# The middle block as one sequence of slots, with the second layer norm and router product inside

## What is computed

```python
x = x + 0.5 * _L0_ffn_ref(_layernorm(x), router_w, w1, w2)
x = x + _L0_attn_ref(_layernorm(x), W_in, conv_w, conv_b, dt_bias, A_log, D, norm_weight, W_out)
x = x + 0.5 * _L0_ffn_ref(_layernorm(x), router_w, w1, w2)
```

```python
zxbcdt = x @ W_in                       # z 512, xBC 512 + 2 * 64, dt 8
xBC = _silu(conv(xBC, conv_w, 4 taps) + conv_b)
dt = softplus(dt + dt_bias); dA = exp(dt * A)
# s = s * dA + dt * x B ; y = C s        over the tokens of a batch row
y = (y + D * x) * _silu(z)
y = y * rsqrt(mean(y * y) + EPS) * norm_weight
return y @ W_out
```

## Time and profile before

| | us |
|---|---|
| median of 3 runs | 1469.66 (1469.64 to 1472.97) |
| profiled execution | 1467.08 |
| its span, first to last instruction | 1465.0 |
| TensorE, DVE, ScalarE, GpSimd busy | 1127.1, 825.2, 573.7, 708.2 |
| mean granted TensorE clock | 0.85 |

### The profile page before, as it was taken

How to read it: one execution, slowest core, us unless ns; L and a number is a source line. 1 busy time by engine, 2 the same in 40 slices (tenths; PEclk the granted TensorE clock), 3 DMA queues, 4 the chain that set the end, 5 groups by cost and what they waited for, 6 DMA issues and landing times. The chain is left out here.

```text
span 1465.0 us, 23436 instructions
## 1 busy us (share of the span) xinstructions
PE 1127.1 (77%) x7002; PEld 940.2 (64%) x7034; DVE 825.2 (56%) x1721; ACT 573.7 (39%) x1375; POOL 708.2 (48%) x673
## 2 busy tenths in 40 slices
PE   3748999999177868686869696978494899999900
PEld 3737999999155746464647475655393799999900
DVE  6883444444266667667676767674448344444433
ACT  2313555555134333434344444353141455555500
POOL 7845555554115454554546363646314555555400
PEclk9999999999677969697969787887655899999965
DMA  7752222222310101010101010000291222222277
GB/s 237 237 215 69 77 77 76 77 78 58 99 33 22 37 12 33 23 32 25 32 26 32 18 36 22 26 8 8 89 318 60 69 78 77 78 77 77 58 226 243
DMA packets 77090, 116.26 MB, mean 79 GB/s; under 512 B 10416, under 2 KB 64192, under 8 KB 75712
## 3 DMA queue, kind: packets, MB, share of 16 engines
q1 hardware_dynamic: 52544, 64.68, 13.4%
q0 software_dynamic: 13824, 37.77, 8.4%
q10 hardware_dynamic: 10624, 12.58, 2.6%
HBM read 70.96 MB, written 44.04 MB: 78 GB/s over the span
## 5 line engine op out<-in xcount | busy, mean ns | idle before, releaser
L405 POOL DMA_INDIRECT ys_d<-xs,row_of x144 | 142.4, 989 | 194.8 <-DVE xs L790 184.3
L779 DVE TENSOR_TENSOR xl<-pT,xh 128x256 fp32r<-128x256 f32 x144 | 61.2, 425 | 210.6 <-ACT xh L485 116.6
L472 ACT ACTIVATE hs<-pH 128x512 f32<-128x512 f32 x144 | 86.2, 598 | 229.0 <-PE pH L582 219.0
L400 POOL DMA_INDIRECT xs<-xn_d,token_of x144 | 141.1, 980 | 52.2 <-issue 42.3
L784 DVE TENSOR_TENSOR h2l<-hs,h2h 128x512 fp32r<-128x512 f32 x144 | 99.9, 693 | 84.2 <-ACT h2h L480 77.8
L1281 PE MATMUL bank<-tri_bf,al 128*128 128x128 bf16 x768 | 62.3, 239 | 56.4 <-ACT ex L1173 56.4
L602 PE MATMUL pY<-w2h,h2h 128*128 x576 | 103.4, 301 | 0.5 <-DVE h2l L784 0.3
L1281 PEld LDWEIGHTS bank<-tri_bf,al 128*128 128x128 bf16 x768 | 52.9, 108 | 68.4 <-ACT ex L1173 65.5
L582 PE MATMUL pH<-w1h,xh 128*128 x288 | 93.1, 405 | 1.9 <-DVE xl L779 1.0
L602 PE MATMUL pY<-w2h,h2l 128*128 x576 | 92.0, 282 | 0.0
L602 PE MATMUL pY<-w2l,h2h 128*128 x576 | 91.7, 281 | 0.0
(11 more groups left out here) (243 smaller groups left out, 2789.5 us busy)
## 6 DMA issues: line engine op xcount, KB each, us to landing
xn_d<-xs SPq DMA_DIRECT2D x16, 512.0 KB, 3.4
m_yg<-ys_d SPq DMA_DIRECT2D x64, 128.0 KB, 2.1
xs<-ys_d SPq DMA_DIRECT2D x16, 512.0 KB, 6.1
wst<-in_L_ffn_w_dram ACTq DMA_DIRECT2D x8, 512.0 KB, 4.8
xs<-in_L_attn_x_dram SPq DMA_DIRECT2D x8, 512.0 KB, 7.0
hs<-in_L_ffn_w_dram ACTq DMA_DIRECT2D x8, 512.0 KB, 5.3
lo_d<-w1l SPq DMA_DIRECT2D x1, 4096.0 KB, 11.1
lo_d<-w2l SPq DMA_DIRECT2D x1, 4096.0 KB, 21.4
```

The source lines that it names most:

```text
L400: pool.indirect_dma_start(out=xg[:, t % NX, :], out_offset=None, in_=xn_d, in_offset=bass.IndirectOffsetOnAxis(ap=token_of[:, t:t + 1], ax ...
L405: pool.indirect_dma_start(out=ys_d, out_offset=bass.IndirectOffsetOnAxis(ap=row_of[:, t:t + 1], axis=0), in_=y[:, t % NX, :], in_offset=No ...
L472: act.activation(r[:, u, :], pH[u][:, :], ACT.Relu).then_inc(relu_done.sem, 1)
```

## The change

In the second FFN the first stage goes: `ffn_block` runs its loads, moments, normalisation, transposes, logits and copies only when `first` is set, and the loads of the low halves of the weights (`load_lo`) stand first in SP's queue. `logits` and `rwT` are kept from the first FFN on.

```diff
+            if not first:
+                for m in range(NA):
+                    load_lo(m)
+            if first:
                 for h in range(NA):
                     load(0, h, False)
...
-            else:
-                with pool.Fori(0, T // (2 * AG)) as j:
-                    pows(j, 0)
-                    pows(j, 1)
```

```diff
+PROJECTED = {3: (2, (0, 1)), 0: (1, (2,)), 1: (1, (3, 4))}
+TAPPED = {0: (1, (0, 1)), 1: (1, (2,)), 2: (1, (3, 4))}
+RX = 14
+LEAD = 10
...
+            for s in SLOTS:
+                first, late = blocks(s, PROJECTED)[:1], blocks(s, PROJECTED)[1:]
+                if live(s):
+                    from_state(s)
+                if live(s - 3):
+                    score(s - 3, s)
+                if live(s - 1):
+                    out_product(s - 1)
+                if live(s):
+                    within(s)
+                    to_state(s)
+                if live(s + 1):
+                    turn_b(s + 1)
+                    turn_xc(s + 1)
+                for B in first:
+                    project(*B, s)
+                if live(s):
+                    turn_y(s)
+                if live(s + 1):
+                    sums(s + 1, 0)
+                if live(s + 9):
+                    turn_x(s + 9)
+                if live(s + 2):
+                    project_z(s + 2)
+                if live(s + 1):
+                    sums(s + 1, 1)
+                for B in late:
+                    project(*B, s)
...
+                if live(s + 9):
+                    project_dt(s + 9)
+                if live(s - 2):
+                    turn_x2(s - 2, s)
```

```diff
+            for s in SLOTS:
+                if live(s):
+                    if not ends(s):
+                        decay_state(s)
+                    add_skip(s)
+                    gate_y(s)
+                if live(s + 1):
+                    scale_x(s + 1)
+                if rooted(s + 1):
+                    powers(s + 1)
+                for G, m in blocks(s, PROJECTED):
+                    if m in BY_POOL:
+                        add_tap(G, m)
```

Operations also change hands or place. ScalarE normalises x and the second norm's x, as scale and bias; DVE makes the bias (`shift`):

```diff
+                act.activation(xn[:, :], xr[:, i % RX, :], ACT.Identity, bias=nmr[:, q, 0:1], scale=rstd[:, q, 0:1]).then_inc(norm_done.sem, 1)
...
+                dve.scalar_tensor_tensor(nmr[:, q, :], mv[:, q, 0:2, 0], -1.0, rstd[:, q, 0:2], ALU.mult, ALU.mult).then_inc(nmr_done.sem, 1)
```

One power of three columns per slot takes the place of two of one column (first norm, second norm, norm of y). GpSimd adds tap 1 for two blocks of five instead of making it for four; DVE does tap 1 for the other three. The bias of dt is added once per group. The mask is made in place, and C B is first copied to SBUF:

```diff
-                dve.tensor_tensor(M[:, :, :], ex[:, :, :], pG.rearrange("p (a t) -> p a t", a=1).to_broadcast([P, H, P]), ALU.mult).then_inc(M_done.sem, 1)
...
+                act.activation(GB[:, :], pGB, ACT.Copy).then_inc(bt_done.sem, 1)
...
+                dve.tensor_tensor(ex[:, :, :], ex[:, :, :], GB[:, 0:P].rearrange("p (a t) -> p a t", a=1).to_broadcast([P, H, P]), ALU.mult).then_inc(M_done.sem, 1)
```

More of the change, by code:

```diff
@@ L513, in _ @@
                 s.open(pe)
[L514 to L538, removed]
-                for m in range(0, NA * AG, 2):
-                    if m + 2 < NA * AG:
-                        turn(m + 2)
-                        turn(m + 3)
-                    score(m)
-                    score(m + 1)
@@ new lines, in live, with blocks, rooted, blocks_before @@
+        def live(i):
+            return 0 <= i < T
+        def blocks(s, table):
+            if s % GC not in table:
+                return ()
+            ahead, places = table[s % GC]
+            G = s // GC + ahead
+            return tuple((G, m) for m in places) if 0 <= G < NG else ()
+        def rooted(s):
+            return live(s + 9) or live(s - 2) or live(s - 1)
+        def blocks_before(s):
+            return sum(len(blocks(n, PROJECTED)) for n in range(-LEAD, s))
+        def ends(i):
+            return (i + 1) % PER == 0
@@ new lines, in score, with within @@
+            def score(i, s):
+                pe.wait_ge(x2T_copied.sem, x2T_copied.done(i))
+                pe.wait_ge(raw_done.sem, raw_done.done(blocks_before(s) - 1))
+                pe.wait_ge(logit_copied.sem, logit_copied.done(i - 1))
+                product(pLog, [(xT2[:, k, :], rwT[:, k, :]) for k in range(KD)]).then_inc(logit_ready.sem, 1)
+            def within(i):
+                pe.wait_ge(xdt_done.sem, xdt_done.done(i))
+                pe.wait_ge(M_done.sem, M_done.done(i))
+                pe.wait_ge(t2_done.sem, t2_done.done(i - 1))
+                for h in range(H):
+                    last = pe.matmul(pY[:, h * HD:(h + 1) * HD], ex[:, h, :], xdt[:, h * HD:(h + 1) * HD], start=True, stop=True)
+                last.then_inc(y_ready.sem, 1)
@@ new lines, in convolve @@
+            def convolve(pieces):
+                for n in range(1, CONV):
+                    for G, m in pieces:
+                        if n == 1 and m in BY_POOL:
+                            dve.wait_ge(tap1.sem, tap1.done(pooled(G, m)))
+                            continue
+                        if n == 1:
+                            dve.wait_ge(tap0.sem, tap0.done(G * NB + m))
+                        elif not (n == 2 and m in BY_POOL):
+                            dve.wait_ge(tap_chain, tapped[G, m])
+                        b = ORDER[m]
+                        a = acc[:, G % 2, b, :]
+                        ins = dve.scalar_tensor_tensor(a, raw[:, b, n:n + GT], cwh[:, b, n:n + 1], a, ALU.mult, ALU.add)
+                        if n == CONV - 1:
+                            ins.then_inc(taps.sem, 1)
+                        else:
+                            ins.then_inc(tap_chain, 1)
+                            tapped[0] += 1
+                            tapped[G, m] = tapped[0]
```

1028 lines of the change are left out of this document (521 added, 507 removed).

## The result

The median is 1379.92 us (1379.43 to 1392.05, 4 executions) against 1469.65 us of before; the ratio is 0.9405, with a 95% interval of 0.9352 to 0.9458. So the change makes the kernel faster by 6%, where 1353 us, 8%, had been forecast. The profiled execution has a span of 1378.1 us (before 1465.0) and a mean granted clock of 0.88 (before 0.85).

A forecast was written before the change was run, and what follows sets the result against it. No engine was taken as full; the middle block's queue order was the limit. From 1467.1 us, 69.4 for the block and 47.1 for the second norm gave 1350.6, with the median's 2.6 us 1353; range 1300 to 1405 (8 in 10).

The forecast's parts named there:

- rival A: Middle block: DVE and TensorE bind in turn, group 62 to 70 us, total 1353 (1327 to 1380); chance 0.50.
- the lead: Ten lead slots before the first state product: it comes at 465 instead of 450.7, cost 14 us, bounds -5 and +25.
- the last slots: End of the block: slots 23 to 26 take 61 us, slots 27 to 31 take 59, the tail 5.
- Second norm, -47.1: Between block and second FFN: the norm stage of 49.5 us goes, iotas and a cast stay, gain 47.1 us.
- Norm inside the block: Per chunk, TensorE gains 0.6 us; per group ScalarE reaches 38 us, GpSimd falls to about 32, neither binding.
- The sums of the slots: Steady part, four slots per group: largest of TensorE, DVE and in-slot loop for each slot, summing to 64 us.
- kinds 3, 0, 1 and 2: Slots by s%4, with differing shares of the next groups' convolution; forecast 16.0, 17.6, 15.4 and 15.1 us.
- The clock, +2 per group: Steady slots: TensorE's waits behind slot 0 lower its clock, some 2 us lost, added once per group: 66 us.
- rival D: Block: waits recur, TensorE falls to the low level once per slot, 2 us each; 1392, up to 1430; chance 0.13.
- B: Block: the queues lose almost nothing, group 58 us, total 1301; chance 0.22.
- E: Block: TensorE stays at the low level, 1.8 times its time, 98 us per group, total 1561, slower; chance 0.04.
- Rival C: Block: GpSimd catches the mask in most slots, 1.2 us each, 4.9 per group, total 1385; chance 0.10.

The follow-up runs named there:

- e1: Changed kernel with the second norm and router product taken out of the slots, back to a stage behind the block; 1395.6 us.
- e3: Changed kernel with useless TensorE products ahead of the dt product, 5 in slots with s%4=0 and 8 in those with s%4=2; 1362.3 us.
- e11: Changed kernel with dt and router's products moved later, plus ten useless products ahead of L1242 in slots with s%4=1; 1344.2 us.
- e6: e3 with four more useless products ahead of the turning of y in slots with s%4=2; 1360.7 us.
- e10: e3 with 12 useless products in place of 8 ahead of the dt product in slots with s%4=2; 1354.1 us.
- e2: Changed kernel with the dt product moved to the next slot, behind the product of y with the output weights; 1374.6 us.
- e8: Changed kernel without GpSimd's product of x and D (D*x zero), with e3's useless products; median 1336.7 us.

## Why the prediction was right, and which term was mis-sized

The measured time lies in the range of 1300 to 1405, and at the very end of rival A's own (1380). What A named, slots set by TensorE and VectorE in turn with a wait that costs the clock, is what was found; the 27 us between forecast and median come in the main from one term, and the errors of the lead and of the last slots, 8 us each, happened to cancel.

- **Second norm, -47.1.** Right: -47.0. The low-half loads start behind the barrier (1008.14 to 1011.74) and cost nothing: from the first reduction to the end of the span it is 367.9 us, 368.9 before. The barrier gave 2 us more than the nothing that was counted.
- **Norm inside the block.** "Neither is the sum that binds" was said of ScalarE and GpSimd and holds. ScalarE has 37.7 us per group, 38 forecast, and GpSimd 37.3, not 32, with its scalings at 1.49 us for 1.04. For TensorE 0.6 us per slot was counted and 0.62 of busy time measured in the last slots (e1); the slots there are 0.84 us longer.
- **Lead.** 465 against 456.9. The ten lead slots cost 6 us more than before, not 14; if the bounds of -5 and +25 are those of the cost, it lies between them, as departures from 465 they are missed by 3 us.
- **The sums of the slots.** 16.0, 17.6, 15.4 and 15.1 us for kinds 3, 0, 1 and 2, 64 in all. At the full level e3 has 16.30, 16.66, 16.75 and 16.07 in slots 19, 16, 17 and 18: 65.8. The sum is 1.8 low. By kind it is off by +0.3, -0.9, +1.4 and +1.0, and slots 13 and 21 of e3, of kind 1, take 17.65, so that 3% is partly luck. The longest kind was to be 0, with 17.6 us of VectorE and 11.6 in kind 1; e3's slots 16 and 17 have 15.95 and 15.38. VectorE's sum was good (57.2; 58.1 per group in the kernel after), as was TensorE's (54.7; 55.8 in slots at 1.00: 13.43, 15.12 and 12.15 in slots 8, 13 and 10, 15.12 in e3's slot 7). e11, with a wholly different split (13.2, 20.0, 13.3 and 19.6), comes to 66.1; that this is the forecast's 66 is chance, as the forecast had 2 us of low level in it.
- **The clock, +2 per group: the term that failed.** Measured is 71.6 - 65.8 = 5.8 us per group. The prediction took one wait per group, and priced it by the products right behind it: "idle 2.59 us, then the pair of z products takes 1.20 us for 0.71", and "some 2 us lost". What follows a wait is not one or two products but some 16 us of them, from 573.79 to 590 in the timeline above, and TensorE, now busy for 90% of the time, has no slack to hide it. Six such slots of 23 are 3.5 to 5.9 us longer than e3's of the same kind at the full level, 29 us together, of the 33 us (5.75 x 5.8) that slots 0 to 22 take beyond e3's 65.8 per group. The step was right, that a wait for VectorE brings TensorE to its low level; the length was taken from two rows instead of from the whole stretch at that level, and the waits right ahead of the low slots were those for `xTl`, not those for the mask and y behind slot 0. The row that had it all was quoted under rival D: in the earlier trace rows the chunk that starts at 605.64 runs low and takes 16.7 us, its fellow k=1 11.7.
- **The rivals.** D (1392 to 1430) was half of the truth: the fall comes in a quarter of the slots, at 5 us, not in each at 2. B was out of reach: even e11, with nearly all slots at the full level, has 66 per group and not 58. E: in the kernel after, the low level never held for two slots in a row; its factor of 1.8 is 1.69 by the rows it names (1.20 for 0.71), which changes its 98 us per group to 92 and nothing else.
- **Rival C, the mask in SBUF.** It did not come: the mask takes between 1.20 and 1.23 us in all 32 cases. The reason given, that GpSimd waits at that time, holds for most of them. In seven, GpSimd's decay of S (L1032) lies beside the mask, and there it is GpSimd that pays: 1.6 to 1.9 us for an operation that takes 1.04 alone, and 2.7 to 2.8 in the three where VectorE's L1550, which also has two inputs in SBUF, stands right ahead of the mask. With the mask's old input in PSUM the same pair left each other alone, 21 times between 450 and 1000. Before, and after:

```profile
621.66 1.22 DVE L1518 TENSOR_TENSOR M<-ex,bank 128x1024 f32<-128x1024 f32 x1 [0.21 <-ACT ex L1173]
621.97 1.04 POOL L1074 TENSOR_TENSOR S<-S,dts 64x512 f32<-64x512 f32 x1
```

```profile
948.57 1.23 DVE L1557 TENSOR_TENSOR ex<-ex,GB 128x1024 f32<-128x1024 f32 x1 [3.11 <-ACT ex L1154]
948.81 1.89 POOL L1032 TENSOR_TENSOR S<-S,dts 64x512 f32<-64x512 f32 x1 [1.59 <-PE bank L1224]
```

So the copy of C B to SBUF did expose the mask, but the cost fell on GpSimd. In the cases read (614.96 and 948.81) GpSimd waited another 0.4 us for VectorE behind it, so that nothing was lost there. What the Trainium skill ("SBUF — State Buffer", section "Who interferes with whom") says of two SBUF inputs agrees with the taps (1.37 for 0.75 us) and with this pair.

- **What was to be seen.** No norm stage, first reduction 2.5 us behind the first iota, VectorE at 81%, taps above 0.75: yes. Period of 66, a clock of 0.9 and kind 0 as the longest: no (71.6, 0.85, and the slots at the low level).

## What to carry over

A slot sum that fills TensorE to 90% is not finished until each wait of TensorE has been followed through: price a wait by the whole stretch at the low level behind it, not by its own length. Where the wait can't be removed, products without a use in its place can be faster than nothing, and where they stand matters (e6 and e10); an order that only shifts the wait (e2) gains little. To tell the level from the waits, set TensorE's busy and idle time of the stretch beside each other: from the kernel after to e11 the idle time stayed at 43 us and the busy time fell by 33. And once TensorE is at its full level, look at what runs beside VectorE's long operations: here one GpSimd product of 1.49 us per slot was worth some 10 us.

## What the runs showed of the hardware that was not expected

- TensorE's clock stayed at the lower of its two levels (1.2 GHz; L1224 takes 2.07 us for 1.12) for some 16 us after a wait of 2.50 us, though it was never idle in that time. The length of the last wait doesn't settle it: behind the same wait of 2.50 us slot 7 starts low, while slot 11 starts at the full level (L1224 in 1.12 us) and has a clock of 0.90. In e3 slots 11, 15 and 19 have the same two waits ahead of them, 1.21 and 0.79 us, and have clocks of 0.74, 0.73 and 1.00.
- VectorE's product of 128x1024 with both inputs in SBUF keeps its 1.21 us beside GpSimd's product of 64x512, which takes 1.89 us in place of 1.04 (948.57 and 948.81 above); with one input in PSUM both keep their times (1.22 and 1.04 us, 621.66 and 621.97).
- One kernel can differ by 19 us from one execution to the next: e8 took 1356.0 us once, at a mean clock of 0.895, and 1336.2 to 1338.5 four times, at 0.909 to 0.914.
- Small operations of VectorE are caught by GpSimd, too: a product of 128x32 took 666 ns on average (L1489, 1.01 us at 515.92 beside GpSimd's scaling) where L1495, of the same shape, took 193. The power's argument (L1449, 128 x 3) took 1.01 us beside GpSimd's scaling in one slot and 0.16 in the next, where GpSimd was idle:

```profile
553.52 1.01 DVE L1449 TENSOR_SCALAR m_ve<-m_mv 128x3 f32<-128x3 f32 x1
...
572.65 0.16 DVE L1449 TENSOR_SCALAR m_ve<-m_mv 128x3 f32<-128x3 f32 x1
```
